# Turning the keys: blocks of 32x32 on VectorE and a trip through DRAM in place of TensorE transposes

## The reference

```
xn = layernorm(x)
q, k, v = xn @ wq.T (16 heads), xn @ wk.T (4 heads), xn @ wv.T (4 heads)   # 128 per head
q, k = rope(q), rope(k)
# causal linear attention with a decay for each head, in chunks:
o_intra = ((q_i @ k_j.T) * decay) @ v_j
o_inter = (q_i * q_decay) @ state
state   = state * block_decay + (k_j * k_decay).T @ v_j
s = o @ wo.T
g = silu(mlp(xn))          # gate, up and down products, weights rounded to fp8
return x + s * g
```

## Time and profile before

| | |
|---|---|
| median of 3 runs | 903.83 us (903.53 to 905.08) |
| the profiled execution | 903.93 us, span 902.1 us |
| PE busy | 894.0 us (99%) |
| DVE, ACT, POOL busy | 632.8, 418.6, 369.1 us |
| granted TensorE clock | 1.00 |
| DMA | 138.55 MB, mean 154 GB/s |

### The profile page before, as it was taken

The page is one execution under the profiler, slowest core; times in us unless marked ns, Lnnn a source line. Parts: engine busy times, 40 slices in busy tenths (PEclk is TensorE's granted clock), DMA queues, the critical chain, the costliest instruction groups (busy, mean ns, idle before and its releaser), DMA issues.

```text
span 902.1 us, 12443 instructions
## 1 busy us (share of the span) xinstructions
PE 894.0 (99%) x4122; PEld 739.2 (82%) x4122; DVE 632.8 (70%) x907; ACT 418.6 (46%) x705; POOL 369.1 (41%) x273
## 2 busy tenths in 40 slices
PE   8999999999999999999999999999999999999998
PEld 5878888888888888888888888888888888888887
DVE  7878652677753256766777867687777677798798
ACT  3443433444433456344465444464544455644542
POOL 1011112122122475535455455364454563654546
PEclk9999999999999999999999999999999999999999
DMA  6792304378750524414333413145243144264472
GB/s 214 207 400 94 105 19 157 140 257 312 295 201 21 210 94 147 168 34 153 139 118 141 179 66 141 49 177 194 82 151 127 48 153 143 113 244 127 176 248 102
DMA packets 51115, 138.55 MB, mean 154 GB/s; under 512 B 4224, under 2 KB 25344, under 8 KB 45696
## 3 DMA queue, kind: packets, MB, share of 16 engines
q1 hardware_dynamic: 51072, 138.00, 42.9%
HBM read 96.04 MB, written 41.94 MB: 153 GB/s over the span
## 4 chain that ended last, share of the span: by engine, by line
PE 96%; DVE 3%; DMA 1%; ACT 0%; issue 0%; SPq 0%; DVEq 0%
PE bank L1275 94%; PE bank L1333 1%; DMA stage<-in_x_nat 1%; PE bank L1295 0%; PE bank L1449 0%; DVE wst L834 0%; DVE tail_sb L1118 0%; DVE tail_sb L1116 0%; DVE d_r L1092 0%; ACT mag L522 0%; DVE acc L1112 0%; DVE fz L851 0%; DVE dn_w L843 0%; DVE o_r L1071 0%; DVE mag L827 0%
## 5 line engine op out<-in xcount | busy, mean ns | idle before, releaser
L1275 PE MATMUL bank<-xn,aw 128*128 128x512 f32 x960 | 229.2, 390 | 0.0
L1220 POOL TENSOR_TENSOR rot<-rot 128x512 f32<-128x512 f32 x80 | 127.0, 1587 | 234.7 <-DVE rot L1006 234.7
L1275 PEld LDWEIGHTS bank<-xn,aw 128*128 128x128 f32 x960 | 179.0, 188 | 37.3 <-issue 0.7
L1275 PE MATMUL bank<-o_r,ow 128*128 128x512 f32 (+1 forms) x792 | 186.2, 385 | 0.2 <-DVE o_r L1071 0.2
L1211 POOL TENSOR_TENSOR d_r<-d_sb,d_r 128x512 fp32r<-128x512 f32 x126 | 165.7, 1341 | 37.1 <-ACT d_r L692 37.0
L1275 PE MATMUL bank<-xn,gu_w 128*128 128x512 f32 x768 | 180.0, 389 | 0.4 <-DVE fz L851 0.4
L1275 PEld LDWEIGHTS bank<-xn,gu_w 128*128 128x128 f32 x768 | 144.1, 188 | 30.9 <-DVE dn_w L843 0.8
L1275 PEld LDWEIGHTS bank<-o_r,ow 128*128 128x128 f32 x792 | 144.3, 188 | 29.0 <-issue 0.6
L1005 DVE TENSOR_TENSOR rot<-bank,rope 128x512 f32<-128x512 f32 x80 | 55.2, 690 | 102.6 <-ACT rot L672 102.5
L671 ACT COPY rot<-bank 64x512 f32<-64x512 f32 x80 | 46.8, 585 | 154.6 <-PE bank L1275 154.3
L692 ACT CAST d_r<-d_sb 128x512 fp32r<-128x512 f32 x128 | 79.0, 621 | 84.6 <-DVE d_sb L1065 62.1
(11 more groups left out here) (87 smaller groups left out, 944.3 us busy)
## 6 DMA issues: line engine op xcount, KB each, us to landing
xn<-xn_split SPq DMA_DIRECT2D x15, 2048.0 KB, 7.7
v_decayed<-vd_split SPq DMA_DIRECT2D x32, 512.0 KB, 3.6
vd_r<-v_decayed SPq DMA_DIRECT2D x16, 1024.0 KB, 7.0
v_r<-v_split SPq DMA_DIRECT2D x16, 512.0 KB, 5.8
wst<-in_mlp_w SPq DMA_DIRECT2D x10, 768.0 KB, 5.1
xn_split<-xn SPq DMA_DIRECT2D x3, 2048.0 KB, 11.3
stage<-in_attn_w SPq DMA_DIRECT2D x4, 1280.0 KB, 6.1
stage<-in_x_nat SPq DMA_DIRECT2D x16, 256.0 KB, 4.8
```

The source lines that it names most:

```text
L1220: pool.tensor_tensor(rot1[:, r % RRING, :], rot1[:, r % RRING, :], rot2[:, r % RRING, :], ALU.add).then_inc(qk_sum, 1)
L1275: last = pe.matmul(dst, a, b, start=start and x == 0, stop=stop and x == len(pairs) - 1)
```

## The change

TensorE's `transpose_k` goes, with `kn_round` on ACT and `kn_rest` on DVE. DVE turns both parts of `k_r` in blocks of 32x32 into a new tile `kt_sb` (`turn_k`, in the place of `kn_rest`). SP stores this tile to DRAM in one transfer of 256 KB, waits for it, and fetches it in four transfers of 64 KB, each to 32 partitions of `kn_r` (`move_k`). `state` waits for these. In `kn_r` the part and the tile of tokens are now the innermost two indices, so `state` reads one element in four as weights. Bank 7 and a wait of `rotate` for the transposes are freed.

```diff
-        kn_r = sb("kn_r", [P, 2, VD, DH], F32R)
+        kn_r = sb("kn_r", [P, NQ, Q4, 2, VD], F32R)
+        kt_sb = sb("kt_sb", [P, NQ, Q4, 2, VD])
...
+            def move_k(n):
+
+                sp.wait_ge(kt_d, 2 * n + 2)
+                sp.dma_start(k_dram, kt_sb[:]).then_inc(k_out, 16)
+                sp.wait_ge(k_out, n * 16 + 16)
+                for c in range(NQ):
+                    sp.dma_start(kn_r[c * Q4:(c + 1) * Q4].bitcast(F32),
+                                 k_dram[:, c].rearrange("(q i) l a j -> i q l a j", q=NQ)).then_inc(kn_in, 16)
...
                         load_v((b + 1) % NB, g + (b + 1) // NB)
+                        move_k(n + 1)
                     if final and b < NB - 1:
                         store_fin(b, 0)
...
+            move_k(0)
             load_xn(0, 1)
...
-            def kn_round(n):
-                act.wait_ge(kt_d, n + 1)
-
-                act.copy(kn_r[:, 0, :, :], kt_ps[:, 0:HALF].rearrange("p (t e) -> p t e", t=VD)).then_inc(kn_hi, 1)
...
-                    if r == RRING:
-                        dve.wait_ge(kt_d, n + 1)
-                    else:
+                    if r > RRING:
                         dve.wait_ge(q_decayed, n * HG + r - RRING)
...
-            def kn_rest(n):
-                dve.wait_ge(kn_hi, n + 1)
-                dve.tensor_tensor(kn_r[:, 1, :, :], kt_ps[:, 0:HALF].rearrange("p (t e) -> p t e", t=VD),
-                                  kn_r[:, 0, :, :].bitcast(F32), ALU.subtract).then_inc(kn_lo, 1)
+            def turn_k(n):
+                dve.wait_ge(qk_lo, n * QK + 1)
+                if_later(n, lambda: dve.wait_ge(kn_in, n * 16 * NQ))
+                for a in range(2):
+                    dve.transpose(kt_sb[:, :, :, a].rearrange("p c l j -> p j c l"),
+                                  k_r[:, a, 0:HALF].bitcast(F32).rearrange("p (j c l) -> p j c l", j=VD, c=NQ)).then_inc(kt_d, 1)
...
-            def transpose_k(n):
-
-                pe.wait_ge(qk_sum, n * QK + 1)
-                if not is_first(n):
-                    pe.wait_ge(o_lo, (n - 1) * NOT + 3)
-                else:
-                    pe.wait_ge(v_lo, NV)
-                for j in range(VD):
-                    last = pe.transpose(kt_ps[:, bass.ts(j, P)], rot1[:, 0, bass.ts(j, P)], ident[:])
-                last.then_inc(kt_d, 1)
-
             def state(n):
 
-                pe.wait_ge(kn_lo, n + 1)
-                if_later(n, lambda: pe.wait_ge(o_lo, n * NOT))
+                pe.wait_ge(kn_in, n * 16 * NQ + 16 * NQ)
+                if is_first(n):
+                    pe.wait_ge(v_lo, NV)
+                else:
+                    pe.wait_ge(o_lo, n * NOT)
                 pe.wait_ge(vd_in, n * 16 + 16)
                 for j in range(VD):
-                    last = products(st_bank(n)[:], [(kn_r[:, a, j, :], vd_r[:, j, c, :]) for a, c in SPLIT],
+                    last = products(st_bank(n)[:], [(kn_r[:, :, :, a, j].rearrange("p q l -> p (q l)"), vd_r[:, j, c, :]) for a, c in SPLIT],
                                     start=(j == 0), stop=(j == VD - 1))
```

More of the change, by code:

```diff
@@ L62 @@
 QK = 1 + HG
+Q4 = 32
+NQ = P // Q4
 VT_AT = {(2, m): 2 * TT + m for m in range(TT)} | {(3, m): 3 * TT + m for m in range(TT)}
@@ L98, in attention_mlp_kernel @@
         xn_dram = nc.dram_tensor("xn_split", (NB, P, 2, KT, S), F32, kind="Internal").ap()
+        k_dram = nc.dram_tensor("k_turned", (P, NQ, Q4, 2, VD), F32, kind="Internal").ap()
         g_dram = nc.dram_tensor("mlp_gate", (KT, P, NB * S), F32, kind="Internal").ap()
@@ L196, in proj_bank @@
             return ([bank[4], bank[5], bank[6], bank[4], bank[5]] if is_first(n) else proj_ps)[tile]
-        kt_ps = bank[7]
         def v_bank(v):
@@ L246, in attention_mlp_kernel @@
         v_in = sem("v_in"); vd_in = sem("vd_in"); state_d = sem("state_d")
-        kt_d = sem("kt_d"); kn_hi = sem("kn_hi"); kn_lo = sem("kn_lo")
+        kt_d = sem("kt_d"); k_out = sem("k_out"); kn_in = sem("kn_in")
         score_d = sem("score_d"); decayed = sem("decayed"); q_decayed = sem("q_decayed")
@@ L704, in projections @@
                         other()
-                    if r == 2:
-                        kn_round(n)
                 for other in beside.get(QK, ()):
@@ L1043, in projections @@
                     if r == 2:
-                        kn_rest(n)
+                        turn_k(n)
                     if r == 2 and tables is not None:
@@ L1439, in project, with state @@
                                             for a, c in SPLIT for k in range(KT)]).then_inc(proj_d, 1)
-            def transpose_k(n):
-                pe.wait_ge(qk_sum, n * QK + 1)
-                if not is_first(n):
-                    pe.wait_ge(o_lo, (n - 1) * NOT + 3)
-                else:
-                    pe.wait_ge(v_lo, NV)
-                for j in range(VD):
-                    last = pe.transpose(kt_ps[:, bass.ts(j, P)], rot1[:, 0, bass.ts(j, P)], ident[:])
-                last.then_inc(kt_d, 1)
-            def state(n):
-                pe.wait_ge(kn_lo, n + 1)
-                if_later(n, lambda: pe.wait_ge(o_lo, n * NOT))
+            def state(n):
+                pe.wait_ge(kn_in, n * 16 * NQ + 16 * NQ)
+                if is_first(n):
+                    pe.wait_ge(v_lo, NV)
+                else:
+                    pe.wait_ge(o_lo, n * NOT)
                 pe.wait_ge(vd_in, n * 16 + 16)
                 for j in range(VD):
-                    last = products(st_bank(n)[:], [(kn_r[:, a, j, :], vd_r[:, j, c, :]) for a, c in SPLIT],
+                    last = products(st_bank(n)[:], [(kn_r[:, :, :, a, j].rearrange("p q l -> p (q l)"), vd_r[:, j, c, :]) for a, c in SPLIT],
                                     start=(j == 0), stop=(j == VD - 1))
@@ L1481, in projections @@
                     project(n, tile, g_edge)
-                    if tile == 2:
-                        transpose_k(n)
                     for other in beside.get(tile, ()):
@@ L1583, in _ @@
             project(0, 2, 0)
-            transpose_k(0)
             down(first + 3)
```

## The result

The changed kernel takes 915.22 us (median of 4 executions, 912.64 to 916.80) against 903.9 us before: the ratio is 1.0118, with a 95% interval of 1.0106 to 1.0130, so it is slower by 10 to 12 us. The forecast was 910.0 us, with a range from 902.5 to 921; the narrower range that the prediction gives for its own case, 907 to 915, is missed by 0.2 us. The profiled execution took 912.64 us, with a span of 910.9 us.

What follows compares the result with a forecast made beforehand. The prediction took PE's instruction list as the bound, busy 99% of the span. From 903.93 us it took 4.2 for removed transposes and added 10.3 for late keys: 910.0 us, range 902.5 to 921.

Steps and rivals of the forecast that it cites:

- its own case: The forecast itself, keys late only in the last group: 910.0 us, range 907 to 915, chance 0.58.
- The gain of 4.2 us: PE's list loses 16 pairs of key transposes at 0.26 us each: -4.2 us, bounds 2.2 and 6.1.
- Steps 1 to 12 on time: Keys through DRAM arrive before state with 3.3 to 3.9 us of cover: term 0.
- The last group: Keys late for state by 1.1, 5.1 and 3.3 us in steps 13, 14, 15: +10.3 us, bounds 0 and 19.
- the output store that stood in for it: Old trace's same-size store, issued at 830.84, landing at 839.4, taken as the key store's landing in step 14.
- The granted clock: It could fall after a 5 us wait of PE; no term given, as an early 2.5 us idle left it at 1.00.
- The weights read one in four: Strided weight loads of state: taken as 0, bounds 0 and 27.7 us.
- DVE's transposes: Two per step at 0.45 us each, +0.5 us per step on DVE, hidden by its idle time: term 0.
- PE is held anyway: In the last group DVE has less cover, but PE waits there for late keys: term 0.
- The sum: Whole kernel: 903.93 - 4.2 + 10.3 = 910.0 us.
- a landing of 5 us: Upper bound for the last key load's landing instead of 2 us, raising the last group's lateness to 19 us.
- doubled weight loads: Rival: strided weight loads of state take twice as long, 3.0 us more, 913 us; chance 0.16, shared with fourfold loads, 938.

Runs made afterwards that it cites:

- e1_no_path: Kernel before without key transposes, their ACT rounding and DVE rest, nothing in their place; state reads unturned k_r, packed: 900.4 us, ratio 0.9953.
- e11_after_again: The changed kernel run once more, nothing altered: 915.46 us, ratio 1.0132.
- e10_fill14: Changed kernel with fourteen matmuls, their result overwritten, ahead of state in steps 14 and 15: 912.66 us, ratio 1.0094.
- e9_turn_only: e1_no_path with state reading every fourth element of k_r and DVE's two transposes per step added, result unused: 904.72 us, ratio 1.0006.
- e3_order: Changed kernel with SP's last-group list reordered, move_k ahead of some output loads and stores: 904.57 us, ratio 1.0000.
- e5_order_edge: e3_order with ACT, at group edges, rounding tile 0 of the next projection weights before its decayed-score roundings: 902.62 us, ratio 0.9984.
- e6_relief: e5_order_edge with DVE's finish of output tile 1 moved to the step's end in the last group: 906.6 us, ratio 1.0027.
- e4_fill: Changed kernel with ten matmuls, their result overwritten, ahead of state in steps 14 and 15: 914.07 us, ratio 1.0099.

## Why the prediction came out as it did

- **The gain of 4.2 us** was 3.9 by the medians of e1_no_path and the kernel before, and 4.1 by their step lengths. Costing the pair by the distance between its neighbours (0.26 us), and not by its shown 0.54 us, was right.
- **Steps 1 to 12 on time.** Right: no wait for keys. A store into a free queue landed after 2.0 us (2.5 to 3.6 forecast), a load of 64 KB after 1.9 (2.0), so there was more cover than counted.
- **The last group.** Right in place and cause; the sum was about 2 to 3 us too high. The landings in the changed kernel, of the transfers issued at 829.36 and 829.84 us:

```profile
v_r<-v_split SPq DMA_DIRECT2D x1, 512.0 KB, 7.8
k_turned<-kt_sb SPq DMA_DIRECT2D x1, 256.0 KB, 8.0
```

  The store lands at 837.8, right behind v_r at 837.2, and the last key 3.3 us after it: both as forecast. The waits of steps 13, 14 and 15 were 0.9, 3.1 and 3.6 us in the first profile, and 1.6, 3.3 and 3.6 in e11_after_again, 7.6 to 8.5 together against 10.3. The step that was mis-sized is step 14, 5.1 forecast (5.4 with the share of the transposes) and 3.1 to 3.3 measured. SP came to its list earlier relative to PE than the old trace has it: v_r was issued 5.5 us after the start of the out projection, 6.3 before (829.72 against 823.43). PE had been held in step 13 by the keys, so a part of that wait was probably credit for the next. From the issue of v_r to the landing of the store it was 8.5 us, where the output store that stood in for it gave 9.7 (829.72 to 839.4): it had been issued later.
- **The granted clock: a term that I set to zero.** It costs 1.6 us for each of the two long waits in e11_after_again, 3.1 us. It and the strided weights are the largest parts of what 915.2 has above 910.0. I argued from an idle stretch of 2.5 us at the start of the kernel that left the clock at 1.00. That was one execution: at the same place, after 2.1 us, the clock fell in the profiles of e1_no_path and e9_turn_only. e10_fill14 shows that it is the idling and not the lateness of the keys: they are at least as late, PE is busy, and the clock doesn't fall.
- **Starting again** behind a wait costs 0.2 to 0.3 us, three times: 0.8 us that no term had.
- **The weights read one in four.** Zero was taken, between bounds of 0 and 27.7 us. The load takes 310 ns, neither the same nor double, and 0.6 us shows directly. The rest, 1.7 us by the medians and 2.2 by step lengths, comes through DVE at two edges, which no price for a weight load could have given. The cacheline rule of the Trainium skill ("SBUF — State Buffer", the note on cachelines under "Door 1: The DMA port swizzle") agrees in its sign, in its half that asks for at least two accesses to a line: at a stride of 16 bytes the load is slower. Its other half, by which 4 fp32 can be strided for free, doesn't hold for this load at exactly four. The page gives no number; measured are 122 ns more per load, of which the row of matmuls hides all but 7.
- **DVE's transposes** were taken at 0.45 us each and are 0.55 to 0.6. That "PE is held anyway" in the last group was right for the changed kernel: the 0.9 us in steps 14 and 15 appear only where the keys are in time (e3_order, e9_turn_only).
- **The sum**, from measured terms, the gain, the stride, the waits, the restarts and the clock in the execution profiled in e11_after_again: 903.9 - 4.1 + 2.8 + 8.5 + 0.8 + 3.1 = 915.0, against its 914.9. So the forecast of 910.0 was right in sign and in its main cause, and two errors partly cancelled: 6.7 us of terms at zero against waits forecast 1.8 us too long (10.3 against 8.5). The wide range holds the result, but it had been built from other causes, a landing of 5 us and doubled weight loads.

With the keys in time, what the change gives is 4.1 us, less 2.8 for the stride and 2 for DVE, so nothing: its ratio in e3_order is 1.0000. SP's order removes the waits, and one ACT instruction moved removes the edges' part: e5_order_edge, 1.5 us below the kernel before. The change as made loses through its place in a full list of transfers and not by its idea, but the most that it could give was 0.5%.

## What to carry to other kernels

Before a small transfer is put on the critical path, list what is issued ahead of it on every queue: here it landed behind all that, and a queue of its own didn't help. A wait of the bound engine costs its length and a short restart, and may cost the clock behind it too, so look for all three in the trace. One idle stretch that left the clock up doesn't show that the next one will. Compare step lengths where medians differ by 1 us: a slow start of the kernel can be in one and not in the other. Where two engines that give way to each other run close to the limit, a shift of 0.07 us can cost 1 us at a place that the change never touches; check the tight places, not only the edited ones.

## What the runs showed of the hardware that I had not expected

- A transfer issued by ACT lands behind one that SP issued 1.3 us earlier (800.0 after 799.2), and four of 64 KB behind 2 MB take 7 to 9 us instead of 1.9.
- After PE was idle for 3.10, 3.42 and 3.46 us the granted clock was 0.50, the lower level, and the next 18 matmuls took 1.6 us longer than behind a wait without a fall. After 2.88 us in another execution it stayed at 1.00. It fell after 1.96 us (e6_relief), 2.10 us (start of e1_no_path) and 2.33 us (e4_fill), and stayed after 2.20 us (e4_fill) and 2.55 us (start of the kernel before).
- Where the clock stays, `state` and the row behind it take 0.2 us longer behind a wait than without one.
- A weight load of 128 columns of f32 at a stride of 16 bytes takes 310 ns against 188, and in a row of matmuls of 512 columns only 7 ns of these 122 are seen.
- A transpose of 128x256 f32 in blocks on DVE takes 0.6 us, two in a row 1.1 us.
- A DVE instruction that reads two operands from SBUF takes 0.69 or 1.81 us beside POOL instructions of 1.3 us; the two cases start 3.73 and 3.80 us after POOL's row.
